# Another order for a prologue: keys first, later statistics behind the first maxima, inverse roots on GpSimd, loads reordered

## What is computed

```python
xn = _layernorm(x, axis=-1)                      # x: (4, 512, 256)
s = _L0_attn_ref(xn, Wq, Wk, Wv, Wo)             # 16 heads, 4 key/value heads, head width 128, causal
g = _silu(_L0_ffn_ref(xn, gate_w, w_gate_up, w_down, shared_gate_up, shared_down))
x = x + s * g

# inside the attention, for queries and keys:
q = q * cos + _rotate_half(q) * sin              # rope
q = q * xscale;  k = k * (1.0 / xscale)
attn = softmax(where(causal, q @ k.T / sqrt(128), -inf));  out = (attn @ v) @ Wo
```

## Time and profile before

| | |
|---|---|
| median of 3 runs | 753.03 us (750.61 to 756.46) |
| the profiled execution | 749.65 us, of it 747.8 us from the first instruction to the last (the span) |
| mean granted TensorE clock | 0.98 |
| busy: TensorE, VectorE, ScalarE, GpSimd | 663.3, 616.8, 457.1, 521.7 us |

### The profile page before, as it was taken

One profiled execution on the slowest core, in us unless ns is written; L12 is line 12 of the kernel. 1 busy time (PEld: TensorE's weight loads), 2 busy tenths in 40 slices (PEclk: granted clock), 3 DMA queues, 4 the chain that ended last, 5 costly groups with the idle time before them and its releaser, 6 DMA issues.

```text
span 747.8 us, 17742 instructions
## 1 busy us (share of the span) xinstructions
PE 663.3 (89%) x5026; PEld 470.4 (63%) x5091; DVE 616.8 (82%) x1737; ACT 457.1 (61%) x1269; POOL 521.7 (70%) x565
## 2 busy tenths in 40 slices
PE   3578879799999999999999999999986789999982
PEld 1256546566766767676676666667664468778761
DVE  7988789789999999899998999989866975445477
ACT  3685636565766657667575675656765756666542
POOL 4677768888888688886888867888654734444474
PEclk9999989999999999999999999999998999999997
DMA  9490000500000000000000000000014754444562
GB/s 308 155 317 26 1 0 2 145 16 15 14 0 14 0 14 14 0 14 0 14 7 7 14 0 14 0 14 14 1 42 147 225 89 128 132 129 133 192 254 84
DMA packets 45747, 50.40 MB, mean 67 GB/s; under 512 B 9906, under 2 KB 39058, under 8 KB 45714
## 3 DMA queue, kind: packets, MB, share of 16 engines
q1 hardware_dynamic: 41602, 39.44, 17.6%
q0 software_dynamic: 3840, 10.52, 4.0%
q10 hardware_dynamic: 272, 0.02, 0.0%
HBM read 31.01 MB, written 18.96 MB: 67 GB/s over the span
## 4 chain that ended last, share of the span: by engine, by line
POOL 40%; issue 19%; PE 16%; DVE 14%; ACT 5%; DMA 4%; POOLq 0%; SPq 0%; DVEq 0%; ACTq 0%
POOL arena L533 16%; POOL arena L520 9%; POOL arena L527 9%; PE bank L1497 6%; PE bank L1537 5%; POOL xs_dram L550 4%; DVE arena L381 2%; ACT arena L733 2%; PE bank L1506 2%; DMA arena<-x 1%; PE bank L1517 1%; DVE arena L1044 1%; DVE arena L1043 1%; DVE s_sb L1216 1%; DVE arena L1069 1%
## 5 line engine op out<-in xcount | busy, mean ns | idle before, releaser
L533 POOL TENSOR_TENSOR arena<-arena,rinv 128x128 f32<-128x128 f32 (+3 forms) x256 | 176.5, 721 | 104.9 <-DVE rinv L1063 104.9
L733 ACT ACTIVATE arena<-bank,nmax 128x512 f32<-128x512 f32 (+3 forms) x256 | 132.5, 534 | 63.8 <-DVE nmax L1057 63.8
L1057 DVE CUSTOM_DVE_ANT_0 bank<-bank,mask_b 128x512 f32<-128x512 f32 (+3 forms) x256 | 118.0, 517 | 13.9 <-issue 13.9
L1341 PE MATMUL bank<-arena 128*128 128x128 f16 (+6 forms) x735 | 113.5, 296 | 9.3 <-POOL arena L527 7.2
L1310 PE MATMUL bank<-xnT_hi,arena 128*128 (+1 forms) x320 | 110.4, 387 | 9.8 <-DVE arena L1044 4.9
L741 ACT CAST arena<-bank 128x512 f16<-128x512 f32 (+1 forms) x192 | 93.1, 521 | 41.7 <-PE bank L1354 40.2
L1370 PE MATMUL bank<-arena 128*128 128x512 f16 (+1 forms) x766 | 116.5, 302 | 0.2
L1069 DVE TENSOR_TENSOR arena<-bank,arena 128x512 bf16<-128x512 f32 (+1 forms) x192 | 109.0, 596 | 3.8 <-ACT arena L741 1.7
L1354 PE MATMUL bank<-ident_f,arena 128*128 128x128 f32 x640 | 92.8, 276 | 19.1 <-DVE arena L1069 12.2
L520 POOL TENSOR_TENSOR arena<-arena 128x512 f32<-128x512 f32 x77 | 98.7, 1282 | 2.5 <-DVE arena L1044 2.2
L1341 PEld LDWEIGHTS bank<-arena 128*128 128x128 f16 (+1 forms) x768 | 65.8, 98 | 49.1 <-issue 7.6
(11 more groups left out here) (150 smaller groups left out, 1251.4 us busy)
## 6 DMA issues: line engine op xcount, KB each, us to landing
xs_dram<-s_sb SPq DMA_DIRECT2D x4, 1548.0 KB, 14.3
arena<-xs_dram SPq DMA_DIRECT2D x48, 128.0 KB, 2.4
stage<-w_gate_up SPq DMA_DIRECT2D x16, 352.0 KB
arena<-ys_dram SPq DMA_DIRECT2D x8, 512.0 KB, 6.5
stage<-w_down SPq DMA_DIRECT2D x16, 176.0 KB
stage<-wq SPq DMA_DIRECT2D x4, 512.0 KB, 8.7
stage<-wo SPq DMA_DIRECT2D x4, 512.0 KB, 7.3
stage<-x SPq DMA_DIRECT2D x1, 2048.0 KB, 10.1
```

The lines of the kernel that those rows point to most:

```text
L533: ins = pool.tensor_tensor(pr, pr, rinv[:, par, qt:qt + 1].to_broadcast([P, (qt + 1) * P]), ALU.mult)
L733: ins = act.activation(probs[par][:, P_AT[qt]:P_AT[qt] + n], score_bank[u][:, col:col + n], ACT.Exp, scale=-1.0, bias=nmax[:, par, qt:qt + ...
L1057: ins = dve.tensor_tensor_reduce(score_bank[u][:, col:col + n], score_bank[u][:, col:col + n], mask_b[:, S - n:S], -1.0, 3e38, ALU.add, AL ...
L1341: ins = pe.matmul(score_bank[u][:, col:col + n_k], qT[a][:, j * S + qt * P:j * S + (qt + 1) * P], kT[m][:, 0:n_k], start=(n == 0), stop=(n ...
```

## The change

- TensorE projects the keys first, then queries 0, 1, 2. It waits for one weight chunk before the keys and for the second before queries 0. In round 0 it asks for three chunks before the first projection and for all four before the values.
- The ropes of VectorE follow that order. `statistics(1)` moves from ahead of the low parts of xnT to behind the first `row_max`; `statistics(2)` and `variances(1)` move to behind the rope and sum of queries 2, and `invert_roots(1)` and `shifts()` behind them.
- ScalarE's two square roots and VectorE's two reciprocals are gone. GpSimd raises the variances to the power -0.5 (`inverse_root`), for batch 0 ahead of all its weights, for the others last in its prologue. VectorE's Newton step stays.
- The second chunk's low part goes from GpSimd to VectorE, the fourth's from VectorE to GpSimd; the third and fourth chunks are cast and split behind the exponentials of the first head, and ScalarE casts the second behind the high parts of xnT.
- ScalarE's `normalise(1)` moves behind the cast of queries 2, so that both `normalise` calls stand together.
- Loads: the rope tables come ahead of x's second and third parts, the constants ahead of the third weight chunk, and the chunks of queries 1 and values change places.

```diff
--- before.py
+++ after.py
@@ -68,7 +68,7 @@
-ITEMS_PROLOGUE = ["q0", "k", "q1", "q2", "q3"]
+ITEMS_PROLOGUE = ["k", "q0", "q1", "q2", "q3"]
 ITEMS_FIRST = ["q0", "v", "x10", "q1", "x11", "x20", "k", "x21", "x30", "q2", "x31", "q3", "logit"]
@@ -344,7 +345,7 @@
-        W_CHUNKS = ["k", "q0", "v", "q1", "q2", "o0", "q3", "o1", "o2", "o3"]
+        W_CHUNKS = ["k", "q0", "q1", "v", "q2", "o0", "q3", "o1", "o2", "o3"]
         N_CHUNKS = len(W_CHUNKS)
@@ -424,13 +425,13 @@
             load_weights(1)
-            load_x(1)
-            load_x(2)
             sp.dma_start(tab[:], rope.rearrange("a p s -> p a s")).then_inc(tab_in, 16)
-            for n in range(2, W_FIRST):
-                load_weights(n)
             for dst, host in ((mask_f, mask), (tri_f, tri), (iota_f[:], iota), (row_id[:], rows), (digit[:], digits)):
                 sp.dma_start(dst, host).then_inc(const_in, 16)
+            load_weights(2)
+            load_x(1)
+            load_weights(3)
+            load_x(2)
             for n in range(W_FIRST, N_CHUNKS):
@@ -503,16 +504,23 @@
         def _(pool):
+            pool.memset(exponent[:], -0.5).then_inc(exponent_set, 1)
             pool.memset(s_sb[:], 0.0).then_inc(zeroed, 1)
...
             pool.memset(mask_b[:, 0:S - P], 0.0).then_inc(mask_zero, 1)
+            def inverse_root(g):
+                pool.wait_ge(var_ready, g + 1)
+                pool.tensor_tensor(rstd[:, LN_TILES[g]], var[:, LN_TILES[g]], exponent[:].to_broadcast([P, LN_TILES[g].stop - LN_TILES[g].start]), ALU.pow).then_inc(rooted, 1)
+
+            pool.wait_ge(exponent_set, 1)
+            inverse_root(0)
+
             def weights_lo(n):
...
-            for n in range(W_FIRST - 1):
-                weights_lo(n)
+            weights_lo(0)
@@ -533,12 +541,15 @@
+            rotate_lo("k", PROLOGUE.rot("k"))
             rotate_lo("q0", PROLOGUE.rot("q0"))
-            rotate_lo("k", PROLOGUE.rot("k"))
             rotate_sum("q1", PROLOGUE.item("q1"))
             rotate_lo("q1", PROLOGUE.rot("q1"))
+            weights_lo(2)
             divide(0, 0)
+            weights_lo(3)
             rotate_lo("q2", PROLOGUE.rot("q2"), ROT_BUF_PROLOGUE)
+            inverse_root(1)
@@ -680,10 +691,6 @@
             act.copy(gate_s[0][:], gate_f[:].rearrange("p c e -> p (c e)")).then_inc(const_cast, 1)
-            def root_of(g):
-                act.wait_ge(var_ready, g + 1)
-                act.activation(root[:, LN_TILES[g]], var[:, LN_TILES[g]], ACT.Sqrt).then_inc(rooted, 1)
-
             def weights_hi(n):
@@ -703,17 +710,13 @@
-            root_of(0)
             weights_hi(0)
-            weights_hi(1)
             for c in range(KC):
...
                 xnT_hi_part(0, c, xnT_bank[c][:])
-            root_of(1)
+            weights_hi(1)
             act.wait_ge(ident_in, 16)
             act.copy(ident_b[:], ident_f[:]).then_inc(const_cast, 1)
-            weights_hi(2)
-            weights_hi(3)
@@ -755,16 +758,18 @@
-            rotate_hi("q0", PROLOGUE.rot("q0"))
+            rotate_hi("k", PROLOGUE.rot("k"))
             act.wait_ge(const_in, 16 * 5)
...
             act.copy(tri_b[:], tri_f).then_inc(const_cast, 1)
-            rotate_hi("k", PROLOGUE.rot("k"))
+            rotate_hi("q0", PROLOGUE.rot("q0"))
             exponentials(0, 0, (0,))
...
             exponentials(0, 0, (1, 2))
+            weights_hi(2)
+            weights_hi(3)
+            rotate_hi("q2", PROLOGUE.rot("q2"), ROT_BUF_PROLOGUE)
             normalise(1)
-            rotate_hi("q2", PROLOGUE.rot("q2"), ROT_BUF_PROLOGUE)
             normalise(2)
@@ -927,7 +932,6 @@
                 dve.wait_ge(rooted, g + 1)
-                then(dve.reciprocal(inv, r))
                 then(dve.tensor_tensor(r, inv, inv, ALU.mult))
@@ -958,11 +962,16 @@
             normalise_first()
-            statistics(1)
             for c in range(KC):
                 xnT_lo_part(0, c, xnT_bank[c][:]).then_inc(xnT_lo, 1)
-            statistics(2)
-            variances(1)
+
+            def second_weights_lo():
+                hi, lo = w_split(1)
+                dve.wait_ge(w_hi, 2)
+                dve.wait_ge(w_lo, 1)
+                dve.tensor_tensor(lo, w_stage(1), hi, ALU.subtract).then_inc(w_lo, 1)
+
+            second_weights_lo()
@@ -1091,21 +1100,20 @@
-            for name in ("q0", "k"):
+            for name in ("k", "q0"):
                 first_rope(name)
...
             first_rope("q1")
-            hi, lo = w_split(W_FIRST - 1)
-            dve.wait_ge(w_hi, W_FIRST)
-            dve.wait_ge(w_lo, W_FIRST - 1)
-            dve.tensor_tensor(lo, w_stage(W_FIRST - 1), hi, ALU.subtract).then_inc(w_lo, 1)
             dve.wait_ge(const_cast, 4)
...
             row_max(0, 0)
+            statistics(1)
+            first_rope("q2", PROLOGUE.rot("k"), (0, 0))
+            first_sum("q2")
+            statistics(2)
+            variances(1)
             invert_roots(1)
             shifts()
-            first_rope("q2", PROLOGUE.rot("k"), (0, 0))
-            first_sum("q2")
@@ -1387,10 +1395,11 @@
+            pe.wait_ge(w_lo, 1)
+            pe.wait_ge(xnT_lo, KC)
+            project(PROLOGUE, "k")
             pe.wait_ge(w_lo, 2)
-            pe.wait_ge(xnT_lo, KC)
             project(PROLOGUE, "q0")
-            project(PROLOGUE, "k")
             project(PROLOGUE, "q1")
@@ -1404,12 +1413,14 @@
                         if rd.first:
-                            pe.wait_ge(w_lo, W_FIRST)
+                            pe.wait_ge(w_lo, W_FIRST - 1)
                         if not rd.last:
...
                             weigh_values(rd, -1)
+                        else:
+                            pe.wait_ge(w_lo, W_FIRST)
                         project_values(rd)
```

3 lines of the change are left out of this document (2 added, 1 removed).

## The result

The changed kernel takes **763.1 us** (median of 4 runs, 760.01 to 765.99), the kernel before, run beside it, 752.59: a ratio of 1.0133, 95% interval [1.0074, 1.0191]. Timed once more among the experiments it gave 760.11 us and 1.0100 [1.0063, 1.0137]. So it is slower by 1.0 to 1.3%. The prediction had 758.9 us in a range of 752.5 to 764; the first timing lies near the upper end, because one term of the sum was too small and a loss to TensorE's clock was not in it.

A forecast was written before the change was run, and what follows sets the result against it. It took a queue of VectorE work, held up by GpSimd, to bound the prologue; 749.65 + 5.9 = 755.6 for the profiled execution, put on the median 3.4 above it: 758.9 us, range 752.5 to 764.

The forecast's parts named there:

- a power of over 1 us: Sign of being wrong: GpSimd's power lasting 0.2 or over 1 us; the forecast took 0.5 us.
- a half clock that reached into the scores of head 2: Sign of being wrong: TensorE, quiet from 36 to 44 us, running on at half clock through head 2's scores.
- What bounds the prologue: Prologue: a queue of VectorE work (busy 9.69 of 10 us from 10 to 20), held up in three places by GpSimd instructions.
- The front edge: Prologue start to first score: power 0.5 us, normalisations from 7.97, fourth held to 11.0, keys' rope 16.3, scores at 24.0.
- the lead: First score 2.6 us earlier: 2.72 statistics and 0.9 aggregation moved out, 1.4 blocking avoided, 1.3 new VectorE idle time.
- Where the lead is lost: Late prologue: second power last in GpSimd's queue, shift at 39.6 instead of 31.96, `probs_hi` +6.2, net +5.9 us.
- The term that was too small: GpSimd's power in the prologue: 0.5 us taken, between bounds of 0.24 and 1.5 us.
- The clock: TensorE, quiet from 36 to 44 us, might run on at half clock; listed as a sign, given no size.
- B: Rival, chance 0.18: the power is dear, start-up of up to 4 us at the front edge; +8.4 in total, 761.3 us.
- Its variant of 1.5 us for each power: All four first normalisations behind 10.86 (+1.2) and 1.0 at the second power: +8.1 us.
- C: Rival, chance 0.15: round 0 absorbs 3.3 us of VectorE's waits for ScalarE's casts; +2.6, 755.6 us.
- D: Rival, chance 0.08: the 2.6 us by which scores start earlier survive and the kernel ends faster, 750.4 us.

## Why the prediction came out as it did

The way of the change and where its loss arises were right; the size was too small by one term of the sum, and the clock came on top. I had given a time within 1% a chance of 0.72 and one more than 1% slower 0.26: with 1.0133 the first timing fell in the second case, and with 1.0100 the second one on the border. Two of the signs that I had named for being wrong came up: a power of over 1 us, and a half clock that reached into the scores of head 2 (from 49.27).

**What bounds the prologue: right.** VectorE's queue and the GpSimd instructions beside it. The sum of query 2 was held (1.71 us), the statistics beside GpSimd weren't (2.70 us for eight at 33.06, under GpSimd's 32.55 to 35.75).

**The front edge: right in kind, 1.0 us short.** Four normalisations held to 11.78 (forecast 11.0), rope of the keys released by TensorE at 17.44 (16.3), scores at 24.97 (24.0). The rope table was in time, query 0's sum wasn't held. The start: the power took 1.05 us, 0.55 more than I gave it, so the normalisations started at 8.54 instead of 7.97; only the first was in ahead of GpSimd's subtraction at 8.86, and three, not one, ended behind it (10.99). That is 0.8 us at 11.78 and carries through to the first score. My list of what the lead is made of leaves out a term: as it stands it adds up to 3.7 us, and only with the 1.3 us for the second chunk's low part, which I had in the walk, does it come near the 2.6 that I gave. Measured, the lead was 0.2 at the first rope (17.44 against 17.64) and the 1.4 of the sum that wasn't held.

**Where the lead is lost: right.** The second power was last in GpSimd's queue and ScalarE idled for 8.67 us behind it (forecast 6), released by the shift, with VectorE idle for 3.35 in front of its second correction (forecast 2). Removing one part at a time shows the place of the statistics as the larger cause (1.0057 by itself, lag 7.0, of it 1.28 a table load that the changed kernel doesn't have); the power on top of it shows in the traces alone.

**The term that was too small is the price of the power.** I took 0.5 us for both. Four columns took 1.05, twelve 2.28: a straight line through these two sizes has 0.15 us a column and 0.44 beside them (1.23 for eight more). My bounds, 0.24 and 1.5, held for the first; the second lies outside, because I had priced four columns and not twelve. The chain of the sum with measured terms: division at 32.55 instead of 31.5 (+1.05, from the front edge), the power 1.78 longer: VectorE starts at 41.2 instead of 38.4, ScalarE at 42.45 instead of 39.6. 5.9 + 2.85 = 8.75, and head 1 measured 8.9. Without the power the late statistics left 5.8 by the estimate above, where the sum without its 0.5 has 5.4; so that part of it was near. The variances were held as well (1.13 us instead of 0.17, until GpSimd's subtraction ended at 37.83), which I hadn't seen; it cost nothing, since GpSimd still had the low part of query 2 ahead of the power.

**The clock: named as a risk, not priced.** It came as a half clock between 39.6 and 50 us (0.51; TensorE stood idle until 46.33, for 9.43 us) and cost nothing there, and another at 70 us that cost 1.4. From head 4 on that makes 8.5 + 1.4 = 9.9. The measured difference of the medians was 10.5 in the first timing and 6.8 in the second. That the first is so near to 9.9 is partly luck, as the second shows.

**The rivals.** B (a dear power) was the closest in number to the first timing (761.3; the second lies midway between B and the forecast) and half right: dear, but by its length and not by a start-up of 4 us. Its variant of 1.5 us for each power, +8.1, is nearly what happened (1.05 and 2.28). The first power began 0.15 us behind the variances, at 6.67, and took 1.05 us in all. The Trainium skill (GPSIMD Engine Reference, instruction dispatch) gives about 6 us for a first call of a freshly loaded kernel. No such load appeared in this trace, and that the 763 which I had worked out for a power starting 4 us late equals the first timing is a coincidence. C (round 0 absorbs 3.3 us) fell: the lag from head 1 to head 3 shrank by 0.4, not by 3.3. D fell: the lead was 1.65 and gone by the shift. That the lateness stays behind 50 us was right, but for the 1.4 at 70 us and what the clock added further on.

**What stays open.** How much of the 1.0 to 1.3% is prologue: 8.9 us are 1.2% by the traces, but the second timing as a whole gave 6.8 us. The profiled execution of before lies 3.6 us under the median timed beside it, which makes up that difference; where a usual execution of before loses these 3.6 us is not shown. Why the clock dips at 70 us in some kernels and not in others stays open as well: TensorE was busy for 2.7 us of the 5 before it both in the changed kernel and in the run with 36 more matmuls, where it did not dip. The order of the loads was only tried together with the rest, but for the rope table's wait in the run of the late statistics.
